# A two-network graph kernel: a second bank for transposes, GpSimd widens one piece, and short steps go ahead of widening

## The chip, the cores and the metric

The kernel runs on one NeuronCore of a Trainium2 chip. The metric is device time in microseconds. The kernel before was timed three times: 1000.74, 1003.56 and 1001.58 us, median 1001.58.

## The reference

There are 6250 nodes with 64 features and 206,250 directed edges (each of 100,000 random pairs in both directions, and one loop per node), sorted by destination. `segment_sum(x[src], dst)` sums over each node's incoming edges.

```python
h = relu(layernorm(x))
agg = segment_sum(h[src], dst);  h = relu(relu((h + agg) @ W1 + b1) @ W2 + b2)
agg = segment_sum(h[src], dst);  x = x + relu((h + agg) @ W3 + b3) @ W4 + b4
h = relu(layernorm(x))
y = relu(relu(h[src] @ WM1 + bM1) @ WM2 + bM2) @ WM3 + bM3
z = segment_sum(y, dst)
out = x + relu(relu(concat(h, z) @ WU1 + bU1) @ WU2 + bU2) @ WU3 + bU3
```

Hidden widths are 128, outputs 64. All is float32.

## The kernel before, in words

Nodes lie in 49 windows of 128. The phase `build` (up to about 410 us) counts the edges between each pair of windows into 128 x 128 tables in fp8, uses them for the first sum, and stores them in DRAM as `edge_counts`. The phase `net`, in which the whole change lies, does the rest. Its work goes by blocks of four windows: 13 blocks (`BLOCKS`), the last with one window.

**The first network** (W1, W2) runs block by block in a pipeline written out by hand. TensorE's loop (from L901) does in step s: the four transposes of block s into `ps_t` (L907), the product with W1 of block s-1 into `ps_m`, the product with W2 of block s-2 into `ps_hi`, and the transposes back of block s-3 into `ps_lo` (L929). ScalarE applies the relus (L832). VectorE copies the transposed block from `ps_t` to `xT` (`copy0`, L672) and splits the result of block s-3 into a high and a low part, `first` (`split0`: L681 a mask, L683 a cast, L684 a subtraction). Transposes(b) wait for `xt_ready` of b, which is copy0 of block b-1, since both use the one bank `ps_t`. copy0(b) waits for its transposes and for the product that read `xT` before.

**The two passes of sums.** Each block needs seven pieces (`PIECES`) of the count tables, 448 KB of fp8 for four windows. Piece e (0 to 90 for the first pass, `pieces(0)`; 91 to 181 for the second, `pieces(1)`) is loaded by SP's queue into one of four buffers `net_raw`, widened to fp32r into one of three buffers `net_wide` by `grow` (L603 on VectorE, L829 on ScalarE), and used by TensorE as the moving operand of the sums (L946 in the first pass with two outputs, `ps_hi` and `ps_lo`; L963 in the second with one). The table `EXPAND` says who widens: pieces 0, 2, 4, 6 of a block VectorE, 1, 3, 5 ScalarE, with a running count for each engine's semaphore. Widening of piece e waits for the load and for `used`, the sum three pieces before. SP reloads a buffer once the piece four before is widened.

VectorE, ScalarE and TensorE each have a loop over e. In step e VectorE and ScalarE first widen piece e + `AHEAD` (2) if it is theirs, and then do the small steps of the previous block's network, `stage1` in the first pass (the second layer of the first net, the layer norm, and the message network up to y, whose split parts are `second`), `stage2` in the second. The pieces 0 and 1 are widened ahead of the loops: 1 by ScalarE behind its relus, 0 by VectorE in the first network's loop at s = `BLOCKS`, between split0 of block 10 and split0 of block 11. TensorE's first sum waits for piece 0 and for split0 of blocks up to 11.

**The border of the passes.** The last block (12, one window) has its `stage1` in the steps of the second pass's first block. The sum of piece 6 there needs y of block 12 (`y_split`), so the chain relu, W4, norm (L717 to L736), transposes (L993), copy and split (L739 to L750), WM1 (L998), relu, WM2, relu, WM3, y (L757 to L764) has to be through before it. I number the pieces of that block 0 to 6, and those behind it 7, 8 and so on.

**Others.** GpSimd computes tallies of the keys (L643 to L652, seven rounds), which VectorE compares in `compare` at e = 20. VectorE's first work in `net` is the split of the doubled weight WM1 (L662 to L665), which TensorE reads in stage1 of block 0. `ps_f` is a bank for the products with outputs of 64 columns.

## Time and profile before

| | |
|---|---|
| median of three timed runs | 1001.58 us |
| profiled execution, its own time | 999.83 us |
| span of the profile | 998.0 us |
| mean granted TensorE clock | 0.988 |
| TensorE busy (matmuls) | 907.3 us, 91% |
| VectorE, ScalarE, GpSimd busy | 743.3, 619.9, 312.9 us |
| chain that ended last | PE 50%, DVE 6%, ACT 1%, issue 1% |

The span is the profiled part of the execution; the rest of its time lies around it. Busy shares are averages over the build, the first network and the two passes. The page's line of the granted clock shows nines in 38 of 40 slices.

### The profile page before, as it was taken

To read this page: it belongs to the slowest core of one execution; us is meant where nothing else is said; L and a number is where in the kernel's file an instruction comes from. 1 tells how busy PE (TensorE), PEld (TensorE's weight loads), DVE (VectorE), ACT (ScalarE), POOL (GpSimd) and SP (SyncE) were. 2 spreads that over 40 slices of the span, in tenths; PEclk is the share of its full clock that TensorE was granted. 3 is DMA by queue.
4 is the path that set the end of the run, shared out by engine and by line. 5 is a ranking of instruction groups with operands and counts; after the bars stand their busy time and mean duration, and the time that the engine had idled before them with its cause. 6 is when DMAs were issued, how large, how long until landed. Compare 5 with 4: busy or idle time off the path is not lost.

```text
span 998.0 us, 25451 instructions
## 1 busy us (share of the span) xinstructions
PE 907.3 (91%) x11325; PEld 736.2 (74%) x11325; DVE 743.3 (74%) x807; ACT 619.9 (62%) x638; POOL 312.9 (31%) x204
## 2 busy tenths in 40 slices
PE   0159999999999999898999999999999979999995
PEld 0148888888888888545788888888888857777774
DVE  6999999999999999185565566565565566767672
ACT  1558898889888987244344444444444457777772
POOL 5657785858682300499920000000000000000000
PEclk9999999999999999899999999999999999999998
DMA  3024244424443344303444344433442447777761
GB/s 105 15 77 137 89 136 138 135 89 138 142 130 105 116 132 132 107 1 93 120 120 129 114 126 129 119 116 117 116 124 74 117 156 226 226 230 236 234 202 37
DMA packets 81377, 126.86 MB, mean 127 GB/s; under 512 B 9808, under 2 KB 58064, under 8 KB 81136
## 3 DMA queue, kind: packets, MB, share of 16 engines
q1 hardware_dynamic: 78128, 121.98, 39.9%
q0 software_dynamic: 3136, 3.22, 1.5%
q8 instruction: 90, 1.47, 0.6%
q14 instruction: 23, 0.19, 0.1%
HBM read 84.22 MB, written 40.94 MB: 125 GB/s over the span
## 4 chain that ended last, share of the span: by engine, by line
PE 50%; DVE 6%; ACT 1%; issue 1%; DVEq 0%
PE net_ps_hi L946 14%; PE net_ps_lo L946 14%; PE net_ps_hi L963 10%; PE net_ps_m L899 6%; PE net_ps_f L899 3%; DVE net_wide L603 2%; PE net_ps_hi L899 1%; ACT net_wide L829 1%; DVE hT L772 1%; DVE hT L774 1%; PE net_ps_m L998 1%; PE net_ps_t L907 1%; PE net_ps_t L993 1%; PE net_ps_lo L929 0%; DVE net_first L683 0%
## 5 line engine op out<-in xcount | busy, mean ns | idle before, releaser
L402 ACT ACTIVATE build_cnts<-build_ps_cnt 128x784 fp8e4<-128x784 f32 (+1 forms) x400 | 299.2, 820 | 52.7 <-PE build_ps_cnt L464 47.3
L603 DVE CAST net_wide<-net_raw 128x3584 fp32r<-128x3584 fp8e4 (+1 forms) x104 | 202.6, 1948 | 104.9 <-PE net_ps_lo L946 57.1
L829 ACT ACTIVATE net_wide<-net_raw 128x3584 fp32r<-128x3584 fp8e4 (+1 forms) x78 | 235.8, 3022 | 66.7 <-PE net_ps_hi L963 49.6
L946 PE MATMUL net_ps_hi<-net_wide,net_first 128*128 128x512 f32 (+1 forms) x637 | 249.3, 395 | 3.3 <-DVE net_first L684 3.3
L480 PE MATMUL build_ps_out<-build_parts,build_cnts 128*128 128x198 bf16 x2401 | 242.9, 250 | 0.0
L946 PE MATMUL net_ps_lo<-net_wide,net_first 128*128 128x512 f32 (+1 forms) x637 | 241.5, 383 | 0.0
L293 DVE TENSOR_TENSOR build_hot_lo<-build_grid_lo,build_keys_t 128x4096 bf16<-128x4096 bf16 x100 | 228.1, 2281 | 2.1 <-ACT build_keys_t L390 1.6
L480 PEld LDWEIGHTS build_ps_out<-build_parts,build_cnts 128*128 128x128 fp8e4 x2401 | 198.2, 98 | 8.1
L963 PE MATMUL net_ps_hi<-net_wide,net_second 128*128 128x512 f32 (+1 forms) x637 | 160.0, 403 | 2.5 <-ACT net_wide L829 1.6
L464 PE MATMUL build_ps_cnt<-build_hot_a,build_hot_lo 64*128 64x49 bf16 x6272 | 123.8, 184 | 29.6 <-DVE build_hot_a L293 24.3
L204 POOL DMA_INDIRECT build_edges<-in_edges,build_start_i x49 | 121.4, 2478 | 82.7 <-DVE build_hot_a L293 72.7
L464 PEld LDWEIGHTS build_ps_cnt<-build_hot_a,build_hot_lo 64*128 64x128 bf16 x6272 | 99.0, 94 | 65.2 <-issue 27.6
L963 PEld LDWEIGHTS net_ps_hi<-net_wide,net_second 128*128 128x128 f32 x637 | 116.4, 190 | 37.3 <-issue 13.1
L946 PEld LDWEIGHTS net_ps_hi<-net_wide,net_first 128*128 128x128 f32 x637 | 120.5, 189 | 28.6 <-issue 6.3
L946 PEld LDWEIGHTS net_ps_lo<-net_wide,net_first 128*128 128x128 f32 x637 | 120.5, 189 | 24.9 <-issue 2.9
L197 POOL DMA_INDIRECT build_rows<-in_dst_rows,build_row_i x49 | 101.0, 2061 | 30.8 <-DVE build_hot_a L293 13.7
L293 DVE TENSOR_TENSOR build_hot_a<-build_grid_a,build_keys_t 128x1600 bf16<-128x1600 bf16 x100 | 98.2, 982 | 0.0
L832 ACT ACTIVATE net_hid<-net_ps_m,b_L_gnn_bM 128x512 f32<-128x512 f32 (+1 forms) x26 | 17.3, 665 | 78.2 <-PE net_ps_m L998 73.1
L832 ACT ACTIVATE net_hid<-net_ps_m,b_L_gnn_b 128x512 f32<-128x512 f32 (+1 forms) x26 | 17.2, 663 | 67.5 <-PE net_ps_m L899 67.5
L717 DVE TENSOR_TENSOR net_mid<-net_ps_f,b_L_gnn_b 128x256 f32<-128x256 f32 (+1 forms) x13 | 5.3, 409 | 33.5 <-PE net_ps_f L899 33.5
L899 PE MATMUL net_ps_m<-net_xT,w_L_gnn_W 64*128 64x512 f32 (+3 forms) x52 | 27.9, 619 | 1.8 <-DVE net_xT L712 1.3
L862 ACT ACTIVATE net_squares<-net_h 128x256 f32<-128x256 f32 (+1 forms) x13 | 5.3, 406 | 38.3 <-DVE net_h L728 38.3
(145 smaller groups left out, 632.1 us busy)
## 6 DMA issues: line engine op xcount, KB each, us to landing
net_raw<-edge_counts SPq DMA_DIRECT2D x168, 448.0 KB, 3.5
edge_counts<-build_cnts SPq DMA_DIRECT2D x168, 224.0 KB
xres<-in_x SPq DMA_DIRECT2D x1, 1568.0 KB, 6.9
net_raw<-edge_counts SPq DMA_DIRECT2D x14, 112.0 KB, 2.0
out<-xres SPq DMA_DIRECT2D x12, 128.0 KB, 4.2
build_rows<-in_dst_rows,build_row_i POOLq DMA_INDIRECT x49, 4.2
build_edges<-in_edges,build_start_i POOLq DMA_INDIRECT x49, 5.1
edge_counts<-build_cnts SPq DMA_DIRECT2D x7, 112.0 KB
```

What stands on the lines that cost most here:

```text
L197: nc.gpsimd.indirect_dma_start(rows[:, w, :], None, a["dst_rows"], bass.IndirectOffsetOnAxis(ap=row_i[:, w:w + 1], axis=0)).then_inc(rows_ ...
L204: nc.gpsimd.indirect_dma_start(edges[:, w, :, :].rearrange("p e k -> p (e k)"), None, a["edges"], bass.IndirectOffsetOnAxis(ap=start_i[:, ...
L293: ins = v.tensor_tensor(hot[s % HOT_RING][:, :, :].rearrange("p c (k t) -> p c k t", t=2), grid[:, :].rearrange("p (k t) -> p k t", t=2)[: ...
L402: nc.scalar.activation(cnts[u % A_RING][:, 0:n, :, 8 * k:8 * k + 8], ps_cnt[b % CNT_RING][:, 0:n, 0:8 * NW].rearrange("p t (n a) -> p t a ...
L464: last = nc.tensor.matmul(ps_cnt[b % CNT_RING][:, t, j * NW:(j + 1) * NW], hot_lo[s % HOT_RING][e, c, :], hot_a[s % HOT_RING][e, c, 0:NW], ...
L480: last = nc.tensor.matmul(ps_out[w % 2][:, 0:3 * FX], cnts[u % A_RING][:, w % 2, c, :], parts64[:, c, :, :].rearrange("p t f -> p (t f)"), ...
L603: return issue(expanded[e % WIDE_RING][:, 0:n, :, :].rearrange("p w a d -> p (w a d)"), raw[e % RAW_RING][:, 0:n, :, :].rearrange("p w a d ...
L829: expand(act, lambda to, x: nc.scalar.activation(to, x, ACT.Identity), e).then_inc(grown["act"], 1)
L832: nc.scalar.activation(to, ps, ACT.Relu, bias=Bc[name][:, 0:1]).then_inc(done, 1)
L899: return nc.tensor.matmul(*args, start=True, stop=True)
L946: last = nc.tensor.matmul(ps[(b + 1) % 2][:, 0:n * P], first[:, c, lo:lo + H], expanded[e % WIDE_RING][:, 0:n, k, :], start=(c == 0), stop ...
L963: last = nc.tensor.matmul(ps_hi[b % 2][:, 0:n * P], second[:, c, :], expanded[e % WIDE_RING][:, 0:n, k, :], start=(c == 0), stop=(c == NW ...
```

## The change

The bank of `ps_f` becomes a full bank `ps_ft`, of which `ps_f` is a view; the first network's transposes alternate between `ps_t` and `ps_ft` and wait for the copy two blocks before. Piece 0 is widened by GpSimd, ahead of its tallies. The split of WM1 moves to step e = 3 of VectorE's loop. In the steps e = 92 to 97 (1 to 6 of the second pass's first block, `chain`), VectorE and ScalarE do the small steps first and widen piece e + 2 behind them.

```diff
--- before.py
+++ after.py
@@ -515,7 +515,7 @@
 RAW_RING = 4
 WIDE_RING = 3
 AHEAD = 2
-EXPAND = counts_of([("dve", "act")[(e % PIECES) % 2] for e in range(2 * BLOCKS * PIECES)])
+EXPAND = counts_of([("dve", "act")[(e % PIECES) % 2] if e else "pool" for e in range(2 * BLOCKS * PIECES)])
 
 
 def windows(b):
@@ -557,12 +557,14 @@
         ps_hi = [ph.ps(f"ps_hi{i}", [P, 512]) for i in range(2)]
         ps_lo = [ph.ps(f"ps_lo{i}", [P, 512]) for i in range(2)]
         ps_m = ph.ps("ps_m", [P, 512])
-        ps_f = ph.ps("ps_f", [P, 4, F])
         ps_t = ph.ps("ps_t", [P, 512])
+        ps_ft = ph.ps("ps_ft", [P, 512])
+        ps_f = ps_ft[:, 0:4 * F].rearrange("p (w f) -> p w f", f=F)
+        ps_in = (ps_t, ps_ft)
         ps_check = ph.ps("ps_check", [P, 2])
 
         raw_in = [ph.sem(f"raw_in{i}") for i in range(RAW_RING)]
-        grown = {e: ph.sem(f"grown_by_{e}") for e in ("act", "dve")}
+        grown = {e: ph.sem(f"grown_by_{e}") for e in ("act", "dve", "pool")}
         used = ph.sem("piece_used")
         turned, xt_ready, product_a, relu_a, product_b, relu_b, back_out, split_done = (
             ph.sem("mlp0_" + n) for n in ("turned", "xt_ready", "product_a", "relu_a", "product_b", "relu_b", "back_out", "split_done"))
@@ -590,6 +592,8 @@
         def pieces(number):
             return range(number * BLOCKS * PIECES, (number + 1) * BLOCKS * PIECES)
 
+        chain = pieces(1)[1:PIECES]
+
         def nb(e):
             b = (e // PIECES) % BLOCKS
             return min(4, NW - 4 * b)
@@ -637,6 +641,7 @@
                     ins.then_inc(pool_steps, 1)
                     pool.wait_ge(pool_steps, done[0])
 
+                expand(pool, nc.gpsimd.tensor_copy, 0).then_inc(grown["pool"], 1)
                 for i in range(PIECES):
                     w = slice(i * PIECE, (i + 1) * PIECE)
                     inside, source = tagged[:, 0, :, :], tagged[:, 1, :, :]
@@ -659,17 +664,20 @@
                     expand(dve, v.tensor_copy, e).then_inc(grown["dve"], 1)
 
                 v.memset(eps[:, :], 1e-5).then_inc(eps_set, 1)
-                v.tensor_scalar(wm_high[:, :], W["L1_gnn_WM1_twice"][:, :].bitcast(I32), -4096, None, ALU.bitwise_and).then_inc(wm_ready, 1)
-                dve.wait_ge(wm_ready, 1)
-                v.tensor_copy(wm[0][:, :], wm_high[:, :].bitcast(FP32)).then_inc(wm_ready, 1)
-                v.tensor_tensor(wm[1][:, :], W["L1_gnn_WM1_twice"][:, :], wm_high[:, :].bitcast(FP32), ALU.subtract).then_inc(wm_ready, 1)
+
+                def split_weights():
+                    twice = W["L1_gnn_WM1_twice"]
+                    v.tensor_scalar(wm_high[:, :], twice[:, :].bitcast(I32), -4096, None, ALU.bitwise_and).then_inc(wm_ready, 1)
+                    dve.wait_ge(wm_ready, 1)
+                    v.tensor_copy(wm[0][:, :], wm_high[:, :].bitcast(FP32)).then_inc(wm_ready, 1)
+                    v.tensor_tensor(wm[1][:, :], twice[:, :], wm_high[:, :].bitcast(FP32), ALU.subtract).then_inc(wm_ready, 1)
 
                 def copy0(b):
                     n = (windows(b).stop - windows(b).start) * P
                     dve.wait_ge(turned, b + 1)
                     if b:
                         dve.wait_ge(product_a, b)
-                    v.tensor_copy(xT[0:F, 0:n], ps_t[0:F, 0:n]).then_inc(xt_ready, 1)
+                    v.tensor_copy(xT[0:F, 0:n], ps_in[b % 2][0:F, 0:n]).then_inc(xt_ready, 1)
 
                 def split0(b):
                     w = windows(b)
@@ -688,9 +696,6 @@
                         copy0(s)
                     if 0 <= s - 3:
                         split0(s - 3)
-                    for e in pieces(0)[0:AHEAD]:
-                        if s == BLOCKS and EXPAND[e][0] == "dve":
-                            grow(e)
 
                 def stage1(b, i):
                     if 0 <= b < BLOCKS:
@@ -807,8 +812,10 @@
                     dve.wait_ge(checks, 6)
 
                 for e in [*pieces(0), *pieces(1)]:
-                    if e + AHEAD < pieces(1).stop and EXPAND[e + AHEAD][0] == "dve":
+                    if e + AHEAD < pieces(1).stop and EXPAND[e + AHEAD][0] == "dve" and e not in chain:
                         grow(e + AHEAD)
+                    if e == 3:
+                        split_weights()
                     if e == 2 * PIECES + 6:
                         compare()
                     if e == 4 * PIECES:
@@ -820,6 +827,8 @@
                         stage2(b - BLOCKS, i)
                     if e == pieces(1)[PIECES - 1]:
                         stage1(BLOCKS, 0)
+                    if e in chain and EXPAND[e + AHEAD][0] == "dve":
+                        grow(e + AHEAD)
                 for i in range(PIECES):
                     stage2(BLOCKS - 1, i)
 
@@ -883,13 +892,15 @@
                         relu(hid[1][:, 0:n], ps_m[:, 0:n], "L1_gnn_bU2", relu_u2)
 
                 for e in [*pieces(0), *pieces(1)]:
-                    if e + AHEAD < pieces(1).stop and EXPAND[e + AHEAD][0] == "act":
+                    if e + AHEAD < pieces(1).stop and EXPAND[e + AHEAD][0] == "act" and e not in chain:
                         grow(e + AHEAD)
                     b, i = e // PIECES - 1, e % PIECES
                     if b < BLOCKS:
                         stage1(b, i)
                     else:
                         stage2(b - BLOCKS, i)
+                    if e in chain and EXPAND[e + AHEAD][0] == "act":
+                        grow(e + AHEAD)
                 for i in range(PIECES):
                     stage2(BLOCKS - 1, i)
 
@@ -901,10 +912,10 @@
                 for s in range(BLOCKS + 3):
                     b = s
                     if b < BLOCKS:
-                        if b:
-                            pe.wait_ge(xt_ready, b)
+                        if b >= 2:
+                            pe.wait_ge(xt_ready, b - 1)
                         for j, w in enumerate(range(windows(b).start, windows(b).stop)):
-                            last = nc.tensor.transpose(ps_t[0:F, j * P:(j + 1) * P], h0[:, w, :], ident[:, :])
+                            last = nc.tensor.transpose(ps_in[b % 2][0:F, j * P:(j + 1) * P], h0[:, w, :], ident[:, :])
                         last.then_inc(turned, 1)
                     b = s - 1
                     if 0 <= b < BLOCKS:
```

## Rows read from the trace of the kernel before

**Rows 1.** Busy us and count of each engine, then granted clock, DMA share, GB/s.

```profile
407.00:460.00 53.00, 44.60 (x187) 22.83 (x185) 35.56 (x60) 20.29 (x27) 45.23 (x51) 0.93 0.16 53
...
783.00:822.00 39.00, 31.41 (x175) 25.54 (x173) 25.63 (x46) 19.41 (x15) 0.00 (x0) 0.96 0.54 162
```

**Rows 2.** Timeline: start, us, engine, line, what; in brackets the idle time before.

```profile
411.65 0.64 DVE L665 TENSOR_TENSOR net_wm<-w_twice,net_wm_high 128x128 fp32r<-128x128 f32 x1
...
412.22 0.67 DVE L672 COPY net_xT<-net_ps_t 64x512 f32<-64x512 f32 x1
...
412.95 0.63 PE L907 MATMUL net_ps_t<-identity,hT 128*64 128x128 f32 x4 [1.13 <-DVE net_xT L672]
...
416.47 2.07 PE L899 MATMUL net_ps_m<-net_xT,w_L_gnn_W 64*128 64x512 f32 x2
...
421.33 1.21 PE L899 MATMUL net_ps_m<-net_xT,w_L_gnn_W 64*128 64x512 f32 x2
```

**Rows 3.** Windows as in rows 1, where the clock falls and where it rises.

```profile
414.50:415.00 0.50, 0.13 (x1) 0.00 (x0) 0.26 (x1) 0.27 (x1) 0.50 (x1) 0.71 1.09 444
...
817.40:817.60 0.20, 0.20 (x2) 0.20 (x1) 0.00 (x0) 0.00 (x0) 0.00 (x0) 0.79 0.00 0
```

**Rows 4.** Timeline, first network in its steady state.

```profile
430.81 1.10 DVE L683 CAST net_first<-net_high 128x512 fp32r<-128x512 f32 x1
...
433.16 0.36 PEld L907 LDWEIGHTS net_ps_t<-identity,hT 128*64 128x64 f32 x4 [0.37 <-DVE net_xT L672]
```

**Rows 5.** Timeline, end of the first network and the first sum.

```profile
454.84 0.68 DVE L684 TENSOR_TENSOR net_first<-net_ps_lo,net_high 128x512 fp32r<-128x512 f32 x1
...
455.44 2.01 DVE L603 CAST net_wide<-net_raw 128x3584 fp32r<-128x3584 fp8e4 x1
...
457.38 0.68 DVE L681 TENSOR_SCALAR net_high<-net_ps_lo 128x512 int32<-128x512 int32 x1
...
459.26 0.77 PE L946 MATMUL net_ps_hi<-net_wide,net_first 128*128 128x512 f32 x1 [3.30 <-DVE net_first L684]
```

**Rows 6.** Timeline of GpSimd and the comparison; landing of net_raw's loads, 405 to 480.

```profile
411.58 1.36 POOL L643 TENSOR_SCALAR net_tagged<-keys 128x448 f32<-128x448 bf16 x1
...
504.33 0.36 POOL L652 TENSOR_TENSOR net_tally<-net_tagged 128x14 f32<-128x14 f32 x1
...
534.04 0.20 DVE L791 TENSOR_TENSOR net_tally<-net_tally,net_node 128x49 f32<-128x49 f32 x1
...
DMA to landing us min/median/max: 3.2/3.5/5.6
```

**Rows 7.** Timeline, border of the first pass's blocks 0 and 1.

```profile
483.33 1.15 POOL L648 TENSOR_TENSOR net_tagged<-net_tagged 128x448 f32<-128x448 f32 x1
...
483.36 3.00 DVE L603 CAST net_wide<-net_raw 128x3584 fp32r<-128x3584 fp8e4 x1 [4.32 <-PE net_ps_lo L946]
...
487.74 1.12 PE L899 MATMUL net_ps_m<-net_xT,w_L_gnn_W 128*128 128x512 f32 x2 [1.31 <-DVE net_xT L712]
```

**Rows 8.** Timeline, border of the two passes.

```profile
801.31 2.02 DVE L603 CAST net_wide<-net_raw 128x3584 fp32r<-128x3584 fp8e4 x1
...
801.43 0.26 ACT L862 ACTIVATE net_squares<-net_h 128x64 f32<-128x64 f32 x1 [0.45 <-DVE net_h L728]
...
803.25 0.21 DVE L731 TENSOR_REDUCE net_stats<-net_squares 128x1 f32<-128x64 f32 x1
...
806.10 0.28 DVE L739 COPY hT<-net_ps_t 64x128 f32<-64x128 f32 x1
...
807.21 2.03 DVE L603 CAST net_wide<-net_raw 128x3584 fp32r<-128x3584 fp8e4 x1
...
809.29 3.18 ACT L829 ACTIVATE net_wide<-net_raw 128x3584 fp32r<-128x3584 fp8e4 x1
...
812.78 0.43 PE L899 MATMUL net_ps_f<-w_L_gnn_WM,net_hid 128*128 128x64 f32 x2 [2.85 <-ACT net_hid L832]
...
814.21 6.59 PE L963 MATMUL net_ps_hi<-net_wide,net_second 128*128 128x512 f32 x21 [1.00 <-DVE net_second L764]
```

## The prediction

> **What bounds the kernel now.** I read the page's chain of waits first: it runs through TensorE nearly everywhere, and its dips into VectorE and ScalarE sit in two seams. So I cut the span into windows there. In the 53 us of the first network (407 to 460) TensorE is busy 44.6 us at a granted clock of 0.93, in the 39 us around the change of passes (783 to 822) 31.4 us at 0.96 [rows 1]. Between and behind the seams the order of work is not touched by the change, apart from later tallies on GpSimd. What can be won lies in about 8.4 + 7.6 us of idle TensorE, plus matmuls at the lower level (1.2 GHz instead of 2.4). Everything below comes from the timelines of these two seams.
>
> **Start of the first network.** Before, transposes(1) wait for copy(0), which starts at 412.22 only when the weight split's last step (411.65, 0.64 us) is off VectorE; the transposes start at 412.95 after 1.13 us idle, the first product behind them [rows 2]. After: copy(0) starts as soon as the first four transposes are done, about 411.9 (0.3 us earlier), and transposes(1) run beside it. Product(0) starts near 412.6; it takes 1.05 us (its two instructions show 1.12 at full clock [rows 7], with some overlap), copy(1) 0.1 + 0.67 behind it, and product(1) starts at 414.5 instead of 416.5, because transposes(2) no longer stand between copy(1) and it. Then the clock matters. It fell to half at about 414.7 [rows 3], after a stretch in which TensorE waited three times, and rose at about 421.4, so that a product took 2.07 us and four transposes twice their time; product(2) started at 421.33 [rows 2]. Three cases, each counted to the end of product(2), which was 422.54:
> - it falls and stays as long: by 421.4 the new order has done product(1) and its partner, transposes and product(2), end 421.5: 1.0 us won;
> - it falls at the same moment but rises after 3.4 us, as it did after the two other falls, where TensorE was busy without a break (817.5 after 814.1) [rows 3]: product(1) ends at 416.4, the next product at about 418.3, transposes and product(2) at 419.8: 2.7 us won;
> - it does not fall: product(2) ends near 418.1: 4.4 us won.
> I take the middle one, since in the new order TensorE has no gap in that stretch: **2.7 us**, ends 1.0 and 4.4.
>
> The Trainium skill (TensorE: Matmul & The Clock Gate, "The HAM clock gate") says that the moment of the change differs from run to run of one kernel. No run shown here tests that; by it any of the three cases could appear in any run of the same kernel.
>
> **Steady state of the first network.** A step of TensorE is two products (2 x 1.05), four transposes out and four back (2 x 0.43, the 0.63 of [rows 2] less a tail of 0.2): 2.96 us. Twice the transposes waited 0.37 us for the copy, one of the two here, because the VectorE cast in front of it took 1.10 us instead of 0.43 [rows 4]. In the new order only the product waits for the copy, and 0.43 us of transposes run meanwhile, so these two waits vanish: **0.6 us**, ends 0 (VectorE falls behind anyway, with 2.5 to 3.2 us of work in a step) and 0.75.
>
> **The first piece off VectorE.** Before: the split of block 10 ends at 455.52, then the widening of piece 0 (2.01 us, 455.44 on) holds up the split of block 11 to 457.38, and the first sum starts at 459.26 when that split is done [rows 5]. After: split 11 starts at 455.54 on the old scale. The sum starts **1.85 us** earlier. Piece 1 (ScalarE, 3.2 us behind its last relu) and piece 2 (VectorE, needed two pieces, 6.4 us, after the start) are in time.
> What it costs on GpSimd: the trace has no copy there. Nearest rows: 448 elements take 1.36 us in a tensor_scalar [rows 6] and 1.15 us in a tensor_tensor [rows 7], so 3584 elements are 9.2 to 10.9 us; from below, 2.0 us as on VectorE. I take 10 us, nearest to the one-input row. Its input lands 3.2 to 5.6 us after the issue at 411.2 [rows 6], so it is done by 425 to 428, 30 us ahead of need. Hidden by the whole network. The tallies behind it move 13 us later, from 504.5 to about 518; the comparison that reads them starts at 534.0 [rows 6]. Hidden as well; if GpSimd took over 29 us more, VectorE would stall there. The SP queue waits for GpSimd's count before it reloads buffer 0 (piece 4): earlier than now. The moved weight split (about 1.1 us on VectorE behind piece 4's widening) lies in VectorE's idle time of the first block, and its reader comes a block later.
>
> The skill's page GPSIMD Engine Reference ("8. Key points") speaks against moving work there while VectorE runs: both share SBUF interfaces, and VectorE's two-port modes and two-input operations collide. The rows agree: a widening of 2.03 us took 3.00 when a GpSimd tensor_tensor of 1.15 us had begun 0.03 us before it [rows 7], and behind that widening TensorE waited 1.31 us [rows 7]. The splits of the first network begin at 422, when the new copy may still run, and the shifted tallies meet other widenings in the first two blocks. This cannot be placed to the microsecond. I take 0 net, with ends of 1.0 us won (the collision at 483 goes) and 1.5 us lost (one more at a split at the end of the network, one at a block's border).
>
> **Second seam, pieces 0 to 6 of the second pass beside the last block's network (one window, short steps).** Up to the centring (801.4) all is as before. Before: VectorE widened piece 4 first (801.31 to 803.33), the sum of squares only began at 803.25, though ScalarE's squares were ready at 801.69 [rows 8]. After:
> - sum of squares 801.76 to 801.97 (0.21), then piece 4 to 804.0; root on ScalarE to 802.3, then piece 5 to 805.5;
> - piece 4's sum starts at 804.05 (it was 803.38: 0.65 us LATER), the transposes behind it at 805.8 instead of 805.1, but VectorE was busy until 806.10 anyway, so the copy out starts at 806.1 as before [rows 8];
> - piece 6's widening now follows that copy and the parts (ready 807.15): 807.15 to 809.15; piece 7's was at 807.21 [rows 8] and now comes at 809.15 to 811.1;
> - piece 5's sum 805.9 to 807.5, product at 807.5, its relu on ScalarE at 807.9 to 808.3, second product to 808.8, relu to 809.2. Before, ScalarE widened piece 8 (809.29, 3.18 us) between the two relus and the last product waited 2.85 us for the second, until 812.78 [rows 8]. Now piece 8 comes behind. The last product is done at 809.7;
> - but VectorE still holds piece 7 until 811.1, so the last y is 811.1 + 0.96 (from 812.78 + 0.47 to 814.21). Piece 6's sum starts at 812.1 instead of 814.21 [rows 8]. **2.1 us**.
> Piece 7 is then the next late thing: without it 1.4 us more. Bounds: 0.5 us if a few waits between engines cost 0.1 us more each and the root and its reader queue behind piece 5; 3.5 us if piece 7's widening waits behind the y.
>
> **Clock at the two seams.** The first sum ran at half clock from about 459.1 to 462.4, and the sum from 814.21 until 817.5 [rows 3, 8]. Both followed long idling: some 5 us with 0.3 us of work before 459.26, 5.5 us with 0.8 us of work before 814.21. After the change these are 3.3 and 4.6 us. Each, if it does not fall, gives 1.65 us more. Taken as 0, since long idle stretches remain; ends 0 and 3.3.
>
> **Sum.** 2.7 + 0.6 + 1.85 + 2.1 = 7.25 us off. The profiled execution took 999.83 us (span 998.0 and 1.8 around it), so 992.6 in its terms. The timed runs have their median 1.75 above it, at 1001.58, and the change touches nothing that would explain or remove that, so the forecast is 1001.58 - 7.3 = 994.3 us.
>
> **Rivals.**
> - More clock: none of the three falls comes. 4.4 + 0.6 + 1.85 + 2.1 + 3.3 = 12.3 us: 989.3. For it: less idling before each. Against: 3.3 and 4.6 us of near-idle are left.
> - VectorE takes the place of the waits: the collision with GpSimd costs 1.5 us in the splits, the start gives 1.0, the steady state 0: 1.0 + 0 + 1.85 + 2.1 - 1.5 = 3.5 us off: 998.1, at the border of what can be told. For it: VectorE is busy 35.6 of the 53 us [rows 1], and almost without pause in the last 10.
> - The second seam does not do what it says: widening behind the steps starves the sums (piece 4 already comes 0.65 us later, piece 6 three us later); gain 0 there instead of 2.1: 996.4.
> - Slower: GpSimd's copy is far slower than its rows. It decides once it runs past 457.4 (43 us, 12 ns an element against 3.0 by [rows 6]), since the first sum waits for it; at 55 us (to 470) the sum starts 11 us later than before; less the second seam's 2.1: about 1010. Against: a factor of four to five over every GpSimd row. For it only that no row has an fp8 input there.
>
> **Chances.** Forecast with its own range 991.5 to 997: 0.70 (with it the third rival's 0.07 mostly). More clock 0.10. VectorE and collisions 0.10. GpSimd slow 0.03. What can be told from no change is 0.3%, 3.0 us: below 998.6 is faster. Of the forecast and the first and third rival nearly all is faster, of the second about half: faster 0.89, same 0.08, slower 0.03. Range 989.8 to 998.4: down to nearly all clock falls gone, up to the collision case.
>
> **What would show it.** In the changed trace: transposes(1) within 0.1 us behind transposes(0), no VectorE release in front of any transposes of the first network; product(1) about 3.3 us after the network's first transposes (it was 5.3); no VectorE widening before the first sum, and that sum 1.9 to 2.0 us after split 10's end; a GpSimd cast of about 10 us; in the second seam ScalarE's two last relus within 1.3 us of each other, VectorE's piece 7 as what the last y waits for, and 2.1 us less from the first sum of pass two to piece 6's. The granted clock at the three places says which case it is. I am wrong if GpSimd's cast ends a wait of TensorE, if the sums of pieces 4 or 5 wait more than 1 us for widening, or if collisions stretch the splits so that the first sum starts less than 3.5 us earlier after the network's start.

## The result and the profile after

The changed kernel takes 991.12 us (median of six, 990.25 to 992.91) against 1001.14 us (six, 998.62 to 1003.56) for the kernel before beside it: ratio 0.9903, 95% interval 0.9889 to 0.9918. That is 10.0 us less; 7.3 were forecast, to 994.3, in a range of 989.8 to 998.4. The change is below 1%, but the interval lies wholly under 1, so it is clear of the noise. In two later comparisons, on two chips, the ratio was 0.9889 (0.9848 to 0.9929) and 0.9905 (0.9874 to 0.9936).

The two profiled executions differ by 7.9 us (998.0 and 990.1 us of span). I cut both at four points: TensorE's first transposes of the first network, its first sum, the first sum of the second pass, and piece 6's sum.

| us | before | after | change | forecast |
|---|---|---|---|---|
| build, up to the first transposes | 411.2 | 411.0 | -0.2 | 0 |
| first transposes to first sum | 48.0 | 41.9 | -6.2 | -5.15 |
| first sum to the second pass's first sum | 335.1 | 336.4 | +1.3 | 0 |
| that to the sum of piece 6 | 19.9 | 17.55 | -2.3 | -2.1 |
| piece 6's sum to the end | 183.8 | 183.2 | -0.6 | 0 |

The start of the first network, after (timeline: start, length, engine, line, what, idle before), answers to [rows 2]:

```profile
411.00 0.60 PE L918 MATMUL net_ps_t<-identity,hT 128*64 128x128 f32 x4 [1.23 <-PEq L162]
...
411.44 0.60 PE L918 MATMUL net_ps_ft<-identity,hT 128*64 128x128 f32 x4
411.64 0.68 DVE L680 COPY net_xT<-net_ps_t 64x512 f32<-64x512 f32 x1 [0.55 <-PE net_ps_t L918]
412.38 1.12 PE L910 MATMUL net_ps_m<-net_xT,w_L_gnn_W 64*128 64x512 f32 x2 [0.34 <-DVE net_xT L680]
...
414.43 1.09 PE L910 MATMUL net_ps_m<-net_xT,w_L_gnn_W 64*128 64x512 f32 x2 [0.37 <-DVE net_xT L680]
414.67 3.17 POOL L607 CAST net_wide<-net_raw 128x3584 fp32r<-128x3584 fp8e4 x1 [3.37 <-DMA net_raw<-edge_counts]
...
416.95 1.12 PE L910 MATMUL net_ps_m<-net_xT,w_L_gnn_W 64*128 64x512 f32 x2
```

Read the lengths: products of 1.1 us, not 2.07. The clock did not fall here. Product(2), the third one, ends 7.1 us behind the first transposes (11.3 before), so this place gave 4.25 us. GpSimd's cast took 3.17 us, not 10.

The end of the first network, after, answers to [rows 5]:

```profile
448.86 3.37 POOL L655 TENSOR_TENSOR net_tagged<-net_tagged 128x448 f32<-128x448 f32 x5
449.21 1.06 DVE L691 CAST net_first<-net_high 128x512 fp32r<-128x512 f32 x1
450.19 0.68 DVE L692 TENSOR_TENSOR net_first<-net_ps_lo,net_high 128x512 fp32r<-128x512 f32 x1
450.98 0.69 DVE L689 TENSOR_SCALAR net_high<-net_ps_lo 128x512 int32<-128x512 int32 x1
...
452.88 0.77 PE L957 MATMUL net_ps_hi<-net_wide,net_first 128*128 128x512 f32 x1 [1.56 <-DVE net_first L692]
```

Split follows split with no widening between, but three casts in a row met GpSimd's tallies (0.95 to 1.06 us each). The clock around the first sum, after (a window, then busy us of each engine with its count, granted clock, DMA share, GB/s), answers to [rows 3]:

```profile
452.00:452.50 0.50, 0.00 (x0) 0.00 (x0) 0.50 (x2) 0.00 (x0) 0.42 (x2) 0.72 0.00 0
458.50:459.00 0.50, 0.50 (x3) 0.34 (x2) 0.00 (x0) 0.00 (x0) 0.50 (x1) 0.50 0.24 69
459.00:459.50 0.50, 0.50 (x4) 0.41 (x2) 0.00 (x0) 0.22 (x1) 0.50 (x1) 0.96 0.00 0
```

It fell at 452.2, in the gap, and came back at 459.0: the sums ran 6.2 us at 1.2 GHz after the first had begun (452.88), where they had run 3.2 us before (459.26 to 462.5). Half the difference is 1.5 us, about the 1.3 us of the table's third line.

The border of the passes, after, answers to [rows 8]:

```profile
796.67 0.22 DVE L736 TENSOR_REDUCE net_stats<-net_squares 128x1 f32<-128x64 f32 x1 [0.32 <-ACT net_squares L871]
796.80 2.02 DVE L607 CAST net_wide<-net_raw 128x3584 fp32r<-128x3584 fp8e4 x1
...
800.90 0.28 DVE L744 COPY hT<-net_ps_t 64x128 f32<-64x128 f32 x1 [1.75 <-PE net_ps_t L1004]
...
802.02 3.96 DVE L607 CAST net_wide<-net_raw 128x3584 fp32r<-128x3584 fp8e4 x2
...
803.62 0.37 ACT L841 ACTIVATE net_hid<-net_ps_m,b_L_gnn_bM 128x128 f32<-128x128 f32 x1 [0.58 <-PE net_ps_m L910]
803.89 3.18 ACT L838 ACTIVATE net_wide<-net_raw 128x3584 fp32r<-128x3584 fp8e4 x1
804.04 0.43 PE L910 MATMUL net_ps_ft<-w_L_gnn_WM,net_hid 128*128 128x64 f32 x2 [0.46 <-ACT net_hid L841]
805.90 0.22 DVE L762 TENSOR_TENSOR net_mid<-net_ps_ft,b_L_gnn_bM 128x64 f32<-128x64 f32 x1
...
806.86 6.64 PE L974 MATMUL net_ps_hi<-net_wide,net_second 128*128 128x512 f32 x21 [2.38 <-DVE net_second L769]
```

It goes as worked out: piece 8's widening behind the last relu, the product done at 804.5, and VectorE still at pieces 6 and 7 (802.02 to 805.98) before it comes to y.

### The profile page after: what moved, and what is told of

It is laid out like the page before. It is cut to its first block, busy times and chain, and to the rows that moved or that the text cites. A ratio compares the mean times of both kernels' runs of the same rounds, so it can differ in the third digit from the quotient of the medians.

```text
span 990.1 us, 25451 instructions
## 1 busy us (share of the span) xinstructions
PE 905.0 (91%) x11325; PEld 736.1 (74%) x11325; DVE 744.6 (75%) x806; ACT 619.8 (63%) x638; POOL 318.1 (32%) x205
## 4 chain that ended last, share of the span: by engine, by line
PE 51%; DVE 6%; issue 1%; ACT 0%; DVEq 0%
PE net_ps_hi L957 14%; PE net_ps_lo L957 14%; PE net_ps_hi L974 11%; PE net_ps_m L910 6%; PE net_ps_ft L910 3%; DVE net_wide L607 3%; PE net_ps_hi L910 1%; DVE hT L777 1%; DVE hT L779 1%; PE net_ps_m L1009 1%; PE net_ps_t L1004 1%; PE net_ps_lo L940 0%; ACT net_wide L838 0%; PE net_ps_t L918 0%; DVE net_first L691 0%
## 5 line engine op out<-in xcount | busy, mean ns | idle before, releaser
L722 DVE TENSOR_TENSOR net_mid<-net_ps_ft,b_L_gnn_b 128x256 f32<-128x256 f32 (+1 forms) x13 | 5.3, 410 | 33.1 <-PE net_ps_ft L910 33.1
L910 PE MATMUL net_ps_m<-net_xT,w_L_gnn_W 64*128 64x512 f32 (+3 forms) x52 | 26.9, 598 | 2.3 <-DVE net_xT L717 1.1
```

What stands on the lines that cost most here:

```text
L910: return nc.tensor.matmul(*args, start=True, stop=True)
```

## The experiments

Two questions were open: which part gave how much, and whether what the clock did is a property of the kernel. Twelve runs, in three groups on three chips: nine other kernels, the changed one twice more, and the one before once more. On two of these chips the build took up to 13 us longer in some executions (the first transposes lie between 411 and 424 us behind the span's start), so the medians of a group tell little below 0.4%; the stage lengths, which start behind the build, tell much more. "Half clock" lists for each stretch how many us the granted clock was at half: at the start of the first network, around the first sum, at the second seam. Two kinds of such stretches are left out of it: every profile ends with 7 to 14 us at half clock, and four (changed again, one bank, widening first, start filled) have one or two of 3.4 us in the build, where all these kernels but the last are the same.

| kernel | first transposes to first sum | to second pass | sum 0 to sum 6 | half clock | median us | ratio to before (95%) |
|---|---|---|---|---|---|---|
| before | 48.0 | 335.1 | 19.9 | 6.8, 3.4, 3.4 | 1001.1 | 1 |
| before, again | 52.3 | 335.0 | 20.0 | 13.6, 6.8, 6.8 | 1009.3 (one) | |
| changed | 41.9 | 336.4 | 17.6 | 0, 6.8, 3.4 | 991.1 | 0.9903 (0.9889-0.9918) |
| changed, again | 41.5 | 335.3 | 17.6 | 0, 3.4, 3.4 | 1001.4 | 0.9889 (0.9848-0.9929) |
| changed, third | 43.8 | 334.7 | 17.6 | 6.8, 3.4, 6.8 | 1000.0 | 0.9905 (0.9874-0.9936) |
| one bank | 48.4 | 335.8 | 17.6 | 10.2, 3.4, 6.8 | 1001.9 | 0.9919 (0.988-0.9958) |
| VectorE widens piece 0 | 44.3 | 336.8 | 17.6 | 0, 10.2, 3.4 | 1001.9 | 0.9915 (0.9886-0.9944) |
| widening first | 44.2 | 333.1 | 20.1 | 6.8, 0, 6.8 | 1001.2 | 0.9909 (0.9881-0.9938) |
| weight split first | 42.8 | 336.2 | 17.5 | 3.4, 6.8, 3.4 | 993.7 (one) | |
| tallies late | 40.8 | 336.5 | 17.6 | 0, 3.4, 3.4 | 990.3 (one) | |
| gaps filled | 41.4 | 333.1 | 17.5 | 0, 0, 0 | 987.3 | 0.9858 (0.9832-0.9884) |
| all three | 43.5 | 334.9 | 16.2 | 6.8, 0, 0 | 990.3 | 0.9893 (0.987-0.9915) |
| gaps filled, piece 7 behind | 41.4 | 333.1 | 16.2 | 0, 0, 0 | 994.8 | 0.987 (0.9829-0.991) |
| the same, start filled | 41.5 | 333.1 | 16.2 | 0, 0, 0 | 995.6 | 0.985 (0.9814-0.9887) |

Lines 4 and 6 to 8 are one group, lines 9 to 12 one (kernel before there: 1000.22), lines 2, 5, 13 and 14 one (before: 1010.21; 1010.47 in the first group).

**The changed kernel again.** No edit.

> The changed kernel once more, as the base for the three runs beside it. My theory: 9 to 10 us below the kernel before. In the first profile the first network's start won 4.3 us (clock not fallen), its steady state 0.65, the end of the network 1.2, the second seam 2.3, and 1.4 us were given back because the clock stayed low for 6.8 us around the first sum instead of 3.3. If where the clock falls is set by the program, this profile shows the same two stretches at half clock, of 6.8 and 3.4 us. Rival (the stretches move from run to run of one kernel): one of them has another length or is missing, and the place of the first network's start may show one.

The second profile has 3.4 us at half clock around the first sum where the first has 6.8; the third profile, on another chip than the second, has a fall at the start. So the lengths are not set by the program alone. Whether the chip has a part in them these three profiles cannot tell; on one chip the six runs of this kernel have mean clocks of 0.986 to 0.991, so they differ there too.

**One bank.**

```diff
-        ps_in = (ps_t, ps_ft)
+        ps_in = (ps_t, ps_t)
-                        if b >= 2:
-                            pe.wait_ge(xt_ready, b - 1)
+                        if b:
+                            pe.wait_ge(xt_ready, b)
```

> The changed kernel with the second bank undone. My theory: the wait of the transposes for the copy opens gaps at the start again and the clock falls near 414.7; the start loses about 4 us and the steady state 0.6, so 4 to 5 us slower than the changed kernel. Rival (the start was won by taking the weight split off VectorE and by chance of the clock, not by the bank): 0.3 to 1 us slower, transposes waiting but no fall of the clock.

Start of the network in that kernel:

```profile
425.78 1.06 PE L918 MATMUL net_ps_t<-identity,hT 128*64 128x128 f32 x4 [0.78 <-DVE net_xT L680]
426.77 2.07 PE L910 MATMUL net_ps_m<-net_xT,w_L_gnn_W 64*128 64x512 f32 x2
...
429.69 1.06 PE L918 MATMUL net_ps_t<-identity,hT 128*64 128x128 f32 x4 [0.84 <-DVE net_xT L680]
```

The waits are back, the clock is at half for 10.2 us and the stage is 6.5 to 6.8 us longer than in the first two profiles of the changed kernel. In the medians only 0.4 us is to be seen, and its twelve runs show why: four lie at 1011 to 1012 us with a mean granted clock of 0.981 to 0.983, eight at 998 to 1005 with 0.987 to 0.992. So the bank has a small part that comes back whenever it is undone (the waits, by my estimate from the timelines 1.3 to 1.8 us at the start; and 26.5 instead of 25.4 us from the end of product(2) to the start of product(11)) and a larger one that it wins only in some runs. That it makes low clocks rarer is what the runs say: a mean clock of 0.983 or less stands in four of these twelve, and in none of the 44 timed runs of the changed kernel, of the two kernels that follow here and of the comparison itself (lowest 0.984). That the fall at the start is what becomes rarer is likely (all three one-bank profiles have one there, four of eleven two-bank profiles do), not shown: only one of the four slow runs has a trace, and in it the build too ended late (424.4) and had two falls. My theory's 4 to 5 us is wrong as a figure for the median; the rival's "no fall" is wrong too.

**VectorE widens piece 0 again.**

```diff
-EXPAND = counts_of([... if e else "pool" for e in ...])
+EXPAND = counts_of([... for e in ...])
-                expand(pool, nc.gpsimd.tensor_copy, 0).then_inc(grown["pool"], 1)
                     if 0 <= s - 3:
                         split0(s - 3)
+                    if s == BLOCKS:
+                        grow(0)
```

> The changed kernel with piece 0 widened by VectorE again, between the splits of blocks 10 and 11. My theory: 1.2 to 2.0 us slower: the cast of 2.0 us returns in front of the last split, and what it costs is that less the collisions with GpSimd's tallies, which shift by 3.2 us. Rival (the gap before the first sum also sets the length of the low clock): the longer gap moves the fall so that it is shorter, as in the kernel before (3.3 instead of 6.8 us), which gives back 1.7 us: no difference to be seen.

```profile
457.48 2.01 DVE L607 CAST net_wide<-net_raw 128x3584 fp32r<-128x3584 fp8e4 x1
...
459.42 0.68 DVE L688 TENSOR_SCALAR net_high<-net_ps_lo 128x512 int32<-128x512 int32 x1
...
462.05 0.77 PE L958 MATMUL net_ps_hi<-net_wide,net_first 128*128 128x512 f32 x1 [3.96 <-DVE net_first L691]
```

The stage is 2.4 to 2.7 us longer: 1.94 us of widening; the rest lies beside two casts of the last splits that took 1.21 and 1.17 us as GpSimd's tallies ran, which I read as collisions. The size is above the 1.2 to 2.0 us that I gave. The low clock did not get shorter with the longer gap, it was 10.2 us here, so this profile speaks against the rival; but since these lengths differ between profiles of one kernel, one profile does not settle it, and the medians (1001.9 against 1001.4) do not either.

**Widening first at the second seam.**

```diff
-        chain = pieces(1)[1:PIECES]
+        chain = ()
```

> The changed kernel with the order of the second seam undone (widening ahead of the short steps). My theory: 2.1 to 2.3 us slower, all of it between the sums of pieces 0 and 6 of the second pass (17.55 us now, 19.9 then), ScalarE's widening of piece 8 standing between the two last relus again. Rival (the starved sums cost as much as the chain wins, and the 2.3 us come from a later start of the seam): less than 1 us.

```profile
815.62 3.18 ACT L838 ACTIVATE net_wide<-net_raw 128x3584 fp32r<-128x3584 fp8e4 x1
...
819.12 0.69 PE L910 MATMUL net_ps_ft<-w_L_gnn_WM,net_hid 128*128 128x64 f32 x2 [2.85 <-ACT net_hid L841]
...
820.80 1.62 PE L974 MATMUL net_ps_hi<-net_wide,net_second 128*128 128x512 f32 x3 [1.00 <-DVE net_second L769]
```

20.1 instead of 17.55 us, in the same way as in [rows 8], the same waits to 0.01 us: 2.55 us, 0.25 above the theory. That excess is the clock: it had fallen 3 us ahead of piece 6's sum here, and WM3's product took 0.69 us where [rows 8] has 0.43. The medians do not separate it (0.9909 against 0.9889, intervals overlap).

**The weight split first.**

```diff
-                    if e == 3:
-                        split_weights()
+                split_weights()
                 def copy0(b):
```

> The changed kernel with the split of the doubled weight WM1 back at the head of the phase. My theory: the first copy starts 0.3 us later and so does everything up to the first sum; nothing else moves, and 0.3 us cannot be told from no change in the time. If the clock stays up at the start here too, the weight split is not what kept it up. Rival (the weight split is what opened the gaps at the start): the clock falls some 4 us behind the first transposes and the way from them to the first sum is 3 us or more longer than the 41.5 to 41.9 us of the changed kernel.

The first product begins 1.37 us behind the first transposes, as in the changed kernel (1.38): in this profile the split costs nothing, not the 0.3 us I gave it; its last step took 0.28 us where it had taken 0.64 [rows 2]. The clock fell all the same, later than in the one-bank kernels, at 416.3 us, for 3.4 us:

```profile
415.38 1.09 PE L910 MATMUL net_ps_m<-net_xT,w_L_gnn_W 64*128 64x512 f32 x2 [0.37 <-DVE net_xT L682]
416.40 2.08 PE L910 MATMUL net_ps_hi<-net_hid,w_L_gnn_W 128*128 128x512 f32 x2
```

Up to there the order and the gaps are those of the changed kernel. The rival has its fall some 4 us behind the first transposes (4.4), but not its price: the stage is 0.9 to 1.3 us longer than in those two profiles, not 3 or more. One run cannot say whether the split made this fall likelier; the third profile of the changed kernel has a fall there without it.

**Tallies late.**

```diff
                 expand(pool, nc.gpsimd.tensor_copy, 0).then_inc(grown["pool"], 1)
+                pool.wait_ge(x_ready, 1)
-                    if e == 2 * PIECES + 6:
+                    if e == 5 * PIECES + 6:
                         compare()
```

(and the two readers of the comparison three blocks later).

> The changed kernel with GpSimd's tallies held back until the first block's sums are added up, and their comparison moved from e = 20 to e = 41. It takes the collisions out of the first network's splits and the first block. My theory: each cast of the splits takes 0.43 us (they took up to 1.26), the way from the first transposes to the first sum is 0.6 to 0.7 us shorter (41.2 to 41.3 without a fall of the clock), and TensorE waits 0.3 to 0.4 us instead of 1.15 for the first block's sum at the border of blocks 0 and 1: 1.4 us in all. Rival (the casts are long for another reason, for example ScalarE or the loads): unchanged casts and waits.

The casts of the splits, first in the changed kernel, then here (count, ns minimum/median/maximum):

```profile
L691 DVE CAST net_first<-net_high x13: 226/657/1258, 420.3 to 453.2; 128x512 fp32r<-128x512 f32 x12, 128x128 fp32r<-128x128 f32 x1
```

```profile
L692 DVE CAST net_first<-net_high x13: 227/426/427, 420.5 to 452.2; 128x512 fp32r<-128x512 f32 x12, 128x128 fp32r<-128x128 f32 x1
...
479.52 1.12 PE L911 MATMUL net_ps_m<-net_xT,w_L_gnn_W 128*128 128x512 f32 x2 [0.34 <-DVE net_xT L718]
```

The theory holds where it looked: casts of 0.43 us, a wait of 0.34, and a stage of 40.8 us, somewhat more than the 0.6 to 0.7 us forecast. But what it won was given back. From one block's first product (the row at 479.52) to the next the changed kernel takes 26.1, 26.8, 26.9, 26.9, 26.8 and 26.7 us; here it is 26.0, 26.8, 28.4, 27.2, 26.9 and 27.0, and TensorE waits twice for a split of the short steps, where the changed kernel does once (0.9 us, at the last block):

```profile
PE net_ps_m L1010 <- DVE net_h_parts L756: 2.2, 2, 1.4
```

```profile
552.95 0.74 PE L1010 MATMUL net_ps_m<-net_h_parts,net_wm 128*128 128x512 f32 x2 [1.35 <-DVE net_h_parts L756]
```

The tallies collide with VectorE's short steps of a later block instead: these six periods are 2.1 us longer in all, against 0.7 to 1.1 us won ahead of the first sum and 0.8 at the border of blocks 0 and 1. I had not reckoned with that. It is not peculiar to this edit: wherever an edit shifts the tallies they can land there. In the kernel with one bank and in the one with VectorE's widening TensorE waited 1.45 and 1.13 us for the same kind of split, 48 us behind the first sum, and in the changed kernel not at all there.

**The gaps filled.** Five products read by nobody.

```diff
                     b = s - 3
+                    if b == BLOCKS - 1:
+                        pe.wait_ge(relu_a, BLOCKS)
+                        for _ in range(3):
+                            mm(ps_m[:, :], W["L0_gnn_W2"][:, :], hid[1][:, :])
...
                         stage1(BLOCKS, 0)
+                        for _ in range(2):
+                            mm(ps_m[:, :], W["L0_gnn_W2"][:, :], hid[2][:, :])
                     use2(e)
```

> The changed kernel with five products more on TensorE whose result nobody reads: three in the gap ahead of the first sum, two in the gap ahead of piece 6's sum in the second pass. They fill idle time (1.05 us each) and delay nothing. My theory: what pulls the clock down at the two seams is the idling itself, so neither the first sum nor the sum of piece 6 runs at half clock; the first is worth 1.7 or 3.4 us, the second 1.7: from the first sum to the second pass's first sum 333.4 us instead of 335.3 to 336.4, and 3 to 5 us less in the time. Rival (the clock falls by itself from time to time, in stretches that have nothing to do with the gaps): stretches of 3.4 us or more at half clock at these or other places, no gain.

```profile
449.07 2.74 PE L910 MATMUL net_ps_m<-net_hid,w_L_gnn_W 128*128 128x512 f32 x6
451.65 0.27 PE L944 MATMUL net_ps_lo<-identity,hT 128*128 128x128 f32 x1
452.65 0.47 PE L961 MATMUL net_ps_hi<-net_wide,net_first 128*128 128x512 f32 x1 [0.73 <-DVE net_first L692]
```

```profile
449.00:453.00 4.00, 3.27 (x12) 1.50 (x10) 3.72 (x7) 2.95 (x1) 3.52 (x7) 1.00 0.02 4
785.00:810.00 25.00, 22.09 (x96) 15.73 (x96) 17.80 (x31) 17.36 (x12) 0.00 (x0) 1.00 0.61 183
```

No fall at either seam, 333.1 us to the second pass, and a ratio of 0.9858, four runs of 986.3 to 987.9 with a clock of 0.994 to 0.996. In all four kernels with filled gaps both seams stayed at full clock; of the ten other profiles, the two of before included, nineteen of twenty seams had a fall. At the seams it is the idling that pulls the clock down: filling it is the only edit, and it held in every profile.

**All three.** Tallies late, gaps filled (three and one), and piece 7 behind the y:

```diff
-                    if e in chain and EXPAND[e + AHEAD][0] == "dve":
+                    if e in chain[:-2] and EXPAND[e + AHEAD][0] == "dve":
                         grow(e + AHEAD)
+                    if e == chain[-1]:
+                        grow(e + 1)
```

> The changed kernel with the tallies late, the gaps filled (three products and one), and VectorE's widening of piece 7 behind the last y instead of ahead of it. My theory: 1.4 us from the tallies, 1.0 to 1.4 us from piece 7 (the y follows its product at once, 17.55 us from sum 0 to sum 6 of the second pass become 16.1 to 16.5), 3.4 to 5 us from the clock: 6 to 8 us below the changed kernel, 1.5 to 1.8% below the kernel before. Rival for piece 7 (its sum then waits for the widening what the y won): sum 7 starts as late as before. Rival for the clock as in the run beside it.

990.3 us, 1.1% below the kernel before where I had forecast 1.5 to 1.8%, and 3 us ABOVE the kernel with the gaps filled alone. Sum 6 comes 1.3 us earlier as expected. The late tallies lose as in their own run (the third and fourth period again 28.4 and 27.2 us), and here that is seen without the clock: neither kernel has a fall between the first sum and the second pass, and that way takes 334.9 us against 333.1. And in this profile the clock fell at the start for 6.8 us (2.8 us of the stage). I had added up gains that were not there.

**Once more the changed kernel, the gaps filled with piece 7 behind, the start filled, and the kernel before.** The second leaves the tallies where they are; the third adds, to that, thirteen small matmuls at the start:

```diff
                 use(NU - 1, 0, both(NU - 1) * (NW + 1))
+                pe.wait_ge(totalled, NW - 1)
+                for _ in range(6): ... matmul(ps_out[1][:, 0:3 * FX], ident_b, parts64[:, 0, :, :] ...)
...
+                        # 3 transposes into ps_lo[0] behind transposes(1), 4 behind product(0)
```

> The changed kernel a third time, beside the two that follow. My theory: what varies from run to run is where the clock falls; the time between the first transposes and the first sum is 41.4 to 41.9 us plus half of what lies at half clock there, from the first sum to the second pass's first sum 333.4 us plus half of what lies at half clock there, and sum 0 to sum 6 of the second pass 17.55 us. Rival (other things drift too): these sums miss by over 0.5 us.

> The changed kernel with the gaps filled (three products ahead of the first sum, one ahead of piece 6's sum) and VectorE's widening of piece 7 behind the last y; the tallies stay where they are. My theory: the way from the first sum to the second pass's first is 333.0 us as in the kernel with the gaps filled alone, sum 0 to sum 6 16.2 instead of 17.55 us, so 1.0 to 1.4 us below that kernel and 5 us or so below the changed one: the fastest of all, ratio to the kernel before 0.984 to 0.986. Rival (piece 7's sum waits for its widening and takes the gain back): sum 6 early, but the first product of the next block as late as before.

> The kernel of the run beside it with the gaps at the start of the first network filled too: six small products behind the build's last sum, three transposes ahead of the first product and four behind it, results read by nobody. My theory: the clock then stays up at the start in nearly every run, so the median falls by 0.5 to 2 us and the slowest runs disappear (the two-bank kernels showed a fall there in three of eight profiles, worth 0.8 to 2.9 us). Rival (the idle 1.2 us between the phases, which cannot be filled, is what pulls it down): no difference, the same spread.

> The kernel before, for a second look at its stages. My theory: the parts free of the clock repeat: 45.2 us from the first transposes to the first sum plus half of what lies at half clock there, 333.4 us plus half of that to the second pass, and 19.9 us from sum 0 to sum 6; the stretches at half clock lie at the same three places but not with the same lengths, and at the start always one. Rival (the lengths in the first profile are this kernel's own): 6.8, 3.4 and 3.4 us again.

The changed kernel's stages fit for the sums and the second seam (334.7 is 333.4 and half of 2.8, within 0.1; 17.56 us) but not for the first network: 43.8 us with 7.4 us at half clock, where the rule gives 45.1 to 45.6. The likely reason, not tested, is that at the start part of the low time falls into waits and costs nothing. The kernel before again: 13.6 us at half clock at the start, 52.3 us to the first sum. 45.2 plus half of 15.2 would be 52.8; 335.0 us to the second pass, 1.1 us less than its rule gives. So the rule of half the low time is right to 1 or 2 us only, and the rival, that other things drift too, is not ruled out. Its places of low clock are the same three, the lengths are not.

Piece 7 behind the y:

```profile
806.74 1.08 PE L912 MATMUL net_ps_m<-net_hid,w_L_gnn_W 128*128 128x512 f32 x2
...
807.54 0.22 DVE L769 TENSOR_TENSOR net_second<-net_mid,net_high 128x64 fp32r<-128x64 f32 x1
807.67 2.02 DVE L607 CAST net_wide<-net_raw 128x3584 fp32r<-128x3584 fp8e4 x1
807.90 5.33 PE L980 MATMUL net_ps_hi<-net_wide,net_second 128*128 128x512 f32 x21
```

16.2 instead of 17.55 us, and it stays won: the sum behind the next block's first product follows sum 0 after 22.3 us (23.6 with the gaps filled alone). Its ratio of 0.987, where I had forecast 0.984 to 0.986, and the start-filled kernel's 0.985 cannot be told from each other or from 0.9858; I call none of the three the fastest. The 0.5 to 2 us that I gave to filling the start are not in the medians (995.6 against 994.8). That it keeps the clock up there stays open: its profile shows no fall there and its runs a clock of 0.993 to 0.995, but so do four of the six runs without it.

## Why the prediction was right

**The start of the first network.** The order of events was right, and its third case came (4.4 forecast for it, 4.25 measured), where I had taken the second (2.7). Later profiles of kernels with two banks show falls of 3.4 and 6.8 us there too. This is the term that was furthest off, by 1.55 us, and it has no single size: I had written that any of the cases could appear in any run of one kernel, and three profiles of the changed kernel show two without a fall there and one with 6.8 us. The Trainium skill (TensorE: Matmul & The Clock Gate, "The HAM clock gate") says the same of the moment of the change. I should have put the gain as a mean over cases.

**Steady state.** 0.6 us forecast; from the end of product(2) to the start of product(11) it took 25.4 us instead of 26.1. Right.

**The first piece.** 1.85 forecast, 1.2 measured: from product(11) to the first sum 9.4 us instead of 10.6. The missing 0.6 us lie with the casts of 1.0 us that met the tallies; with the tallies out of the way the stage is 0.7 to 1.1 us shorter. I had set the collisions to 0 net, and the 1.0 us I allowed for the collision at the border of blocks 0 and 1 [rows 7] was not won: the wait there is 1.15 us instead of 1.31, a widening of 2.84 us again. GpSimd's price was off by a factor of three: 3.17 us against 10. It was hidden at either price.

**The second seam.** 2.1 forecast, 2.3 in the first profile, 2.55 when undone, 0.25 of it the clock. VectorE's piece 7 was the next late thing as said (1.4 us named, 1.33 to 1.35 measured).

**The clock at the seams.** I took 0. In the first pair of profiles it was -1.3 us at the first sum and 0 at the second seam: a shorter gap, a longer fall.

**From profile to median.** The sum by profiles was 7.25 forecast, 7.9 measured. That these lie so near each other is in part luck: 1.55 us more at the start and 0.8 us outside the stages of the forecast stand against 0.65 us less at the first piece and 1.3 us lost to the clock around the first sum. The medians differ by 10.0, so 991.1 lies 0.4 us below the 991.5 to 997 that I gave as the forecast's own range and inside the outer range alone. The kernel before's profile had a mean clock of 0.988; its runs beside the later kernels have medians of 0.983 to 0.985 in three groups, while the changed kernel's runs have medians of 0.988 to 0.991 and its first profile 0.990. 0.004 of 1000 us are 4 us of full-speed time in which the clock was missing, of which a part falls into waits. The second profile of the kernel before is such an execution: a mean clock of 0.983, and 4.2 us more in the first network, where the clock was at half for 13.6 instead of 6.8 us. So I started from a lucky execution of the kernel before: it was 1.3 us faster than its median, and the changed kernel's profile 0.8 us slower than its own; with the 7.9 of the profiles that makes the 10.0. That the lucky part is the clock is what these clocks say (in the group whose build did not drift, the eleven runs of the kernel before go from 998.6 us at 0.989 to 1004.7 at 0.982); it was not separated by an experiment.

**The slower rival** never came near: GpSimd was done at 417.8, 35 us ahead of need. The collision rival was half right in its place, at 0.6 us. Of the three falls in the rival with more clock one stayed away and one got longer. The rival at the second seam fell with the run in which that order is undone: it costs 2.55 us there.

## What to carry over

Time the stages of a profile between fixed instructions, not only the whole: here 13 us of drift in a stage that the change does not touch hid an effect of 2.5 us at the second seam that repeats to 0.1 us or, with the clock, 0.3. A gap in which TensorE idles costs itself and then up to half of what follows at the low clock, and this second part varies from run to run; filling the gap with products that nobody reads gave 3 to 5 us here (ratios of 0.9858 against 0.989 to 0.9905, on different chips), a third to a half of what the change gave. Before work on a shared engine is moved out of one stage, look at what it will meet in the next.

## What the runs showed of the hardware

A GpSimd copy of 3584 elements from fp8 to fp32r took 3.17 us (0.88 ns an element), while its tensor_scalar from bf16, also with one input, took 1.35 us for 448 (3.0 ns). The Trainium skill (GPSIMD Engine Reference, "3.1 Elementwise — side-by-side cycle accounting") gives 1.03 cycles an element for simple bodies (its k up to 2); at the 1.2 GHz of its "1. Specifications" that is an estimate of 0.86 ns. The copy agrees, the tensor_scalar is over three times that. I had taken my price from the tensor_scalar.

The granted clock of one and the same kernel fell for different lengths, and at the start of the first network or not, in its three profiles, two of which come from different chips; on one chip the mean clock of the kernel before went from 0.978 to 0.989 in 29 runs. The one thing that kept the clock up at both seams in every profile was to fill the gaps there (four profiles, with 0.7 to 0.9 us of idle time left before the first sum in three of them).
